# A graph network on one core: the turns of full chunks as transposing DMAs in place of TensorE's

## The reference

```python
h = jnp.maximum(_layernorm(x), 0.0)
x = x + _L0_gnn_ref(h, ...)     # 2 sage layers, then log_softmax
h = jnp.maximum(_layernorm(x), 0.0)
x = x + _L1_gnn_ref(h, ...)     # 2 sage layers, 2 linear layers

# layer of block 0:  agg = segment_sum(h[src], dst) / max(deg, 1)
#                    y = concatenate([h, agg]) @ W + b      128 -> 256 -> 128
# layer of block 1:  relu(mean @ W_l.T + b_l + x @ W_r.T)   128 -> 256 -> 256 -> 256 -> 128
```

## Time and profile before

| | |
|---|---|
| median of 3 runs | 588.14 us (587.84 to 588.85) |
| profiled execution | 587.56 us, span 585.7 us |
| PE | 544.2 us busy, 93% |
| DVE | 225.0 us, 38% |
| ACT | 202.9 us, 35% |
| SP's DMA queue | 27.91 MB, 17.6% of 16 DMA engines |

### The profile page before, as it was taken

One profiled execution on the slowest core, in us unless ns is written; L12 is line 12 of the kernel. 1 busy time (PEld: TensorE's weight loads), 2 busy tenths in 40 slices (PEclk: granted clock), 3 DMA queues, 4 the chain that ended last, 5 costly groups with the idle time before them and its releaser, 6 DMA issues.

```text
span 585.7 us, 9420 instructions
## 1 busy us (share of the span) xinstructions
PE 544.2 (93%) x3078; PEld 291.5 (50%) x3078; DVE 225.0 (38%) x500; ACT 202.9 (35%) x368; POOL 24.7 (4%) x36
## 2 busy tenths in 40 slices
PE   1367999999999999999999999999999999999996
PEld 0244655555554654445455555644545445454555
DVE  6899959577775217667411111110000001010001
ACT  1688858567664304455422222200000010100011
POOL 4410000000000000110100000000000000000000
PEclk9997999999999999999999999999999999999999
DMA  3800103010010124333121111232011212111011
GB/s 94 196 1 1 38 1 117 2 36 17 17 35 17 24 70 112 90 90 77 39 76 53 52 52 39 67 117 52 19 35 39 49 35 52 35 35 52 17 32 30
DMA packets 31372, 29.47 MB, mean 50 GB/s; under 512 B 4894, under 2 KB 30879, under 8 KB 31215
## 3 DMA queue, kind: packets, MB, share of 16 engines
q1 hardware_dynamic: 29622, 27.91, 17.6%
q10 hardware_dynamic: 1561, 0.84, 0.6%
q0 software_dynamic: 160, 0.33, 0.2%
HBM read 19.68 MB, written 9.39 MB: 50 GB/s over the span
## 4 chain that ended last, share of the span: by engine, by line
PE 87%; DVE 5%; ACT 3%; DMA 2%; issue 2%; POOL 1%; ACTq 0%; SPq 0%; DVEq 0%; POOLq 0%
PE ps L1036 54%; PE ps L1053 22%; PE ps L990 6%; PE ps L1308 2%; DVE hs_b L493 2%; PE ps L1046 1%; PE ps L1270 1%; DMA hs_b<-self_d 1%; DMA adj<-key_d,adj 1%; ACT adj L1490 1%; POOL adj L1375 1%; PE ps L1242 1%; DVE adj L1426 1%; DMA adj<-in_dst_dram 0%; ACT adj L844 0%
## 5 line engine op out<-in xcount | busy, mean ns | idle before, releaser
L1036 PE MATMUL ps<-adj,hs_b 125*128 (+2 forms) x1050 | 203.6, 351 | 0.0
L1036 PE MATMUL ps<-adj,hs_a 125*128 (+2 forms) x700 | 158.5, 353 | 0.0
L1036 PEld LDWEIGHTS ps<-adj,hs_b 125*128 125x128 f16 x1050 | 96.3, 97 | 103.9 <-issue 6.6
L493 DVE TENSOR_TENSOR hs_b<-iota,hs_b 128x1024 f16<-128x1024 f16 x150 | 95.4, 685 | 27.9 <-PE ps L990 26.9
L844 ACT ACTIVATE adj<-ps 125x500 f32 (+2 forms) x150 | 80.0, 544 | 22.8 <-PE ps L990 16.6
L990 PE MATMUL ps<-hs_b 128*128 128x125 f16 x625 | 68.5, 233 | 20.7 <-DVE hs_b L493 13.1
L990 PEld LDWEIGHTS ps<-hs_b 128*128 128x128 f16 x625 | 46.5, 103 | 65.7 <-DVE hs_b L493 34.4
L1036 PEld LDWEIGHTS ps<-adj,hs_a 125*128 125x128 f16 x700 | 58.5, 98 | 38.8 <-issue 5.4
L975 ACT ACTIVATE actT<-ps,col 128x500 f32<-128x500 f32 (+1 forms) x14 | 8.9, 633 | 148.0 <-PE ps L1053 148.0
L791 DVE TENSOR_TENSOR hs_a<-ps,hs_a 125x512 f32<-125x512 f32 (+1 forms) x7 | 4.4, 634 | 128.9 <-PE ps L1308 128.9
L1053 PE MATMUL ps<-aggT,wts 128*128 128x500 f32 (+1 forms) x112 | 44.6, 540 | 0.4 <-ACT aggT L957 0.4
(11 more groups left out here) (150 smaller groups left out, 356.4 us busy)
## 6 DMA issues: line engine op xcount, KB each, us to landing
invc<-inv_d SPq DMA_DIRECT2D x24, 250.0 KB, 3.3
h_d<-actT SPq DMA_DIRECT2D x6, 500.0 KB, 3.1
wts<-h_d SPq DMA_DIRECT2D x6, 500.0 KB, 4.0
self_d<-hs_b SPq DMA_DIRECT2D x6, 250.0 KB, 2.1
hs_b<-self_d SPq DMA_DIRECT2D x6, 250.0 KB, 3.5
hs_b<-in_x_dram SPq DMA_DIRECT2D x6, 250.0 KB
x_d<-hs_b SPq DMA_DIRECT2D x6, 250.0 KB
hs_a<-x_d SPq DMA_DIRECT2D x6, 250.0 KB
```

Source lines behind the costliest of these rows:

```text
L493: last = nc.vector.tensor_tensor(onehots[slot], iota2.unsqueeze(1).to_broadcast(shape), keys[:, ds(g * 4, 4), :].unsqueeze(2).to_broadcast ...
L1036: last = nc.tensor.matmul(acc[:, 0:n], hs[:, ds(s * (2 * w) + part * w + h * 128, 128)], adj[0:P, ds(c * (S * C) + s * n, n)], start=(isin ...
```

## The change

For the six full chunks of phases 1 and 3, PE, ACT and DVE lose the turns, and SP gets transposing DMAs (`dma_start_transpose`, 2-byte elements):

- Own rows: the rows are first stored to DRAM (`spread`: `hs_d1` in one piece at the start of phase 1; `hs_d3` chunk by chunk along phase 2). `turn_own` reads 512 rows of 128 high values, and 512 of 128 low values, and lands them turned in SBUF; DVE's `own_sum` adds the two into `aggT`. That of chunk c+1 is issued while chunk c is worked on, after `own_sum` of chunk c (one buffer).
- Projected rows of phase 1: ACT writes the high half as f16 into `z16[0]`, DVE the low half into `z16[1]` (`z_low`), and SP turns 4 tiles of 128x128 of each into `hs_b`: 8 DMAs per chunk.
- Activations of phase 3: ACT copies `actT` into a f16 buffer `h16` (2 instructions), SP turns it in 8 DMAs of 128x128; when these have landed DVE writes `actT - h16` into the same buffer, and SP turns that in 8 more. When those have landed, ACT may write the next chunk.

The small chunk 6 stays on PE. The waits for the rows in `source` become waits for the landings (`p1_zin`, `p3_in`).

```diff
+            def turn_own(ph, c, hd, into):
+                for k in range(2):
+                    sp.dma_start_transpose(into[k], hd[ds(c * C, 512), k * D:(k + 1) * D]).then_inc(sem(f"p{ph}_hT"), 16)
...
@@ SP, before the chunks of phase 1 @@
+            if not slow:
+                sp.wait_ge(sem("n_low"), S // PIECE)
             spread(1, ha, D, hs_d1)
             load_inv("p1_", 0, True)
+            if not slow:
+                sp.wait_ge(sem("rows"), 16)
+                turn_own(1, 0, hs_d1, turned1)
@@ SP, step1 @@
+                if not slow and nxt:
+                    sp.wait_ge(sem("p1_h0T"), c + 1)
+                    turn_own(1, c + 1, hs_d1, turned1)
                 sp.wait_ge(sem("p1_self"), c + 1)
                 sp.dma_start(self_d[:, ds(c * C, width(full))], selfT[:, 0:width(full)]).then_inc(sem("p1_self_out"), 16)
+                if not slow and full:
+                    sp.wait_ge(sem("p1_zlo"), c + 1)
+                    for t in range(4):
+                        for k in range(2):
+                            sp.dma_start_transpose(hs_b[:, ds(c * (4 * 2 * D) + (2 * t + k) * D, D)],
+                                                   z16[k][:, t * PT:(t + 1) * PT]).then_inc(sem("p1_zin"), 16)
...
@@ SP, phase 2, step2 and behind it @@
+                    sp.wait_ge(sem("p2_low"), c)
+                    sp.dma_start(hs_d3[ds((c - 1) * C, C), :].rearrange("(t p) f -> p t f", p=P),
+                                 ha[:, ds((c - 1) * (4 * 2 * D), 4 * 2 * D)].rearrange("p (t f) -> p t f", f=2 * D)).then_inc(
+                        sem("p2_rows"), 16)
...
+                sp.wait_ge(sem("p2_rows"), 16 * NFULL)
+                turn_own(3, 0, hs_d3, turned3)
...
@@ SP, step3 @@
+                if not slow and nxt:
+                    sp.wait_ge(sem("p3_ownT"), c + 1)
+                    turn_own(3, c + 1, hs_d3, turned3)
                 n = width(full)
                 sp.wait_ge(sem("p3_relu"), 2 * c + 2)
                 sp.dma_start(h3_d[:, :, ds(c * C, n)],
                              actT.rearrange("p (m n) -> p m n", m=2)[:, :, 0:n]).then_inc(sem("p3_h3_out"), 16)
+                if not slow and full:
+                    for k, half in enumerate(("p3_hi", "p3_lo")):
+                        sp.wait_ge(sem(half), c + 1)
+                        for t in range(4):
+                            for m in range(2):
+                                sp.dma_start_transpose(hs_b[:, ds(c * (4 * 2 * H) + (2 * t + k) * H + m * 128, 128)],
+                                                       h16[:, m, t, :]).then_inc(sem("p3_in"), 16)
...
@@ DVE @@
+            def own_sum(ph, c, parts):
+                dve.wait_ge(sem(f"p{ph}_hT"), 32 * c + 32)
+                wait_past(dve, "p1_h1" if ph == 1 else "p3_h3", 2 * c)
+                nc.vector.tensor_tensor(aggT[:, C:2 * C], parts[0][:, 0:C], parts[1][:, 0:C], ALU.add).then_inc(
+                    sem("p1_h0T" if ph == 1 else "p3_ownT"), 1)
...
                 agg_out(c - 1, True)
+                own_sum(1, c - 1, turned1)
...
                 self_out(c - 1, True)
+                z_low(c - 1)
...
             def low3(c, full):
+                if full and not slow:
+                    dve.wait_ge(sem("p3_in"), 256 * c + 128)
+                    for m in range(2):
+                        by_tile = h16[:, m, :, 0:P]
+                        last = nc.vector.tensor_tensor(by_tile, actT[:, m * C:(m + 1) * C].rearrange("p (t n) -> p t n", n=P),
+                                                       by_tile, ALU.subtract)
+                    last.then_inc(sem("p3_lo"), 1)
+                    return
@@ ACT, z_out and step3 @@
+                if full and not slow:
+                    wait_past(act, "p1_zin", 128 * c)
+                    nc.scalar.activation(z16[0].rearrange("p (t n) -> p t n", n=PT)[:, :, 0:P],
+                                         bank(6, n).rearrange("p (t n) -> p t n", n=P), ACT.Identity, scale=zs).then_inc(
+                        sem("p1_zT"), 1)
+                    return
...
+                if by_dma:
+                    act.wait_ge(sem("p3_relu"), 2 * c + 2)
+                    wait_past(act, "p3_in", 256 * c)
+                    for m in range(2):
+                        last = nc.scalar.activation(h16[:, m, :, 0:P], actT[:, m * C:(m + 1) * C].rearrange("p (t n) -> p t n", n=P),
+                                                    ACT.Copy)
+                    last.then_inc(sem("p3_hi"), 1)
+                    return
@@ PE @@
-                own1(c - 1, True)
...
-                turn1(c - 1, True)
...
-            staged(3, [(lambda c: bank(acc3(c, slow)), ha, D, 0)], [(0, own3, 1), (8, hidden3, 1), (0, turn3, 2)],
--                   [(14, turn2, NFULL)], (NFULL - 1, NFULL, NCH), fill=(5, 8))
+            staged(3, [(lambda c: bank(acc3(c, slow)), ha, D, 0)], ([(0, own3, 1)] if slow else []) + [(8, hidden3, 1)] + ([(0, turn3, 2)] if slow else []),
+                   [(14, turn2, NFULL)], (("p2_low", NFULL - 1), ("p2_low", NFULL), ("p2_low", NCH)), fill=(5, 8))
...
-                   [(0, own3, NFULL), (0, turn3, NFULL - 1), (8, hidden3, NFULL), (16, turn3, NFULL)],
-                   (2 * NFULL - 2, 2 * NFULL, 2 * NCH - 1))
+                   [(0, own3, NFULL), (8, hidden3, NFULL), (16, turn3, NFULL)],
+                   (("p3_in", 256 * (NFULL - 1)), ("p3_in", 256 * NFULL), ("p3_low", 1)))
```

More of the change, by code:

```diff
@@ L204, in sage_program @@
         outb = over(hs_a, 9216, 4 * D, F32)[0:P]
+        PT = 128
+        z16 = [zT[:, :].bitcast(F16)[:, k * 4 * PT:(k + 1) * 4 * PT] for k in range(2)]
+        turned1 = [hs_b[:, (20 + 2 * k) * 2 * D:(22 + 2 * k) * 2 * D] for k in range(2)]
+        turned3 = z16
+        h16 = wts[:, 512:1024].bitcast(F16).rearrange("p (m t n) -> p m t n", m=2, n=PT)
         w1v = wts[:, 0:512].rearrange("p (k o) -> p k o", k=2)
@@ L434, in phase @@
                 if slow:
-                    pool.wait_ge(sem(f"p{ph}_rows"), 16)
+                    pool.wait_ge(sem("rows"), 16 * ph)
                 def step(c, full):
@@ L646, in step1 @@
                     build_c(c + 1, nxt, 1, 5)
[L647 to L650 removed]
+                elif nxt is not None:
+                    build_c(c + 1, nxt, 0, 5)
                 self_out(c - 1, True)
+                z_low(c - 1)
                 if nxt is not None:
@@ L681, in dve_layers @@
                 agg_out(NFULL, False)
-                low(NFULL - 1, True)
                 self_out(NFULL, False)
@@ L760, in step3 @@
                     sem("p3_agg_out"), 1)
+                if full and not slow:
+                    own_sum(3, c, turned3)
                 if not first:
@@ L869, in z_out @@
                 act.wait_ge(sem("scale3"), 2)
-                wait_past(act, "p1_turned", c)
+                if full and not slow:
+                    wait_past(act, "p1_zin", 128 * c)
[3 more added lines that the diff above has]
+                    return
+                if slow:
+                    wait_past(act, "p1_turned", c)
+                else:
+                    act.wait_ge(sem("p1_zin"), 128 * NFULL)
                 nc.scalar.activation(zT[:, 0:n], bank(6, n), ACT.Identity, scale=zs).then_inc(sem("p1_zT"), 1)
@@ L883, in step1 @@
             def step1(c, full, nxt, second=False):
-                h0_turned(c - 1, True)
-                if not second:
-                    high(c - 2, True)
                 if nxt is not None:
@@ L927, in act_layers @@
                 step1(NFULL, False, None)
-                high(NFULL - 1, True)
                 whole(NFULL, False)
@@ L954, in step3 @@
                 nt = n // P
-                act.wait_ge(sem("p3_own"), c + 1)
-                wait_past(act, "p3_h3", 2 * c)
-                nc.scalar.activation(aggT[:, C:C + n], bank(3, n), ACT.Copy).then_inc(sem("p3_ownT"), 1)
-                wait_past(act, "p3_turned", 2 * c)
+                by_dma = full and not slow
+                if not by_dma:
+                    act.wait_ge(sem("p3_own"), c + 1 if slow else 1)
+                    wait_past(act, "p3_h3", 2 * c)
+                    nc.scalar.activation(aggT[:, C:C + n], bank(3, n), ACT.Copy).then_inc(sem("p3_ownT"), 1)
+                if slow:
+                    wait_past(act, "p3_turned", 2 * c)
+                else:
+                    wait_past(act, "p3_lo", c)
                 wait_past(act, "p3_h3_out", 16 * c)
@@ L1151, in step1 @@
                 pieces(S - 6, S).then_inc(sem("p1_agg"), 1)
-                if second:
-                    pe.wait_ge(sem("wt"), 5)
-                turn1(c - 1, True)
             if slow:
@@ L1165, in pe_layers @@
                 pe.wait_ge(sem("absw"), 2)
-                pe.wait_ge(sem("p1_rows"), 16)
+                pe.wait_ge(sem("rows"), 16)
                 chunks(pe, slow1)
@@ L1189, in slow_step, with ready @@
                         p(c, full)
+                def ready(k):
+                    name, value = source[k]
```

(9 more changed lines are left out.)

66 lines of the change are left out of this document (41 added, 25 removed).

## The result

The changed kernel takes 694.17 us (median of 4 runs, 692.62 to 697.55), the kernel before 588.50 in the same comparison (4 runs, 587.84 to 589.78): a ratio of 1.180, 95% interval 1.175 to 1.185. The forecast was 645 us and slower; the direction was right, most of the loss stands where it was put (phase 3), and the size was 49 us short.

The account below looks back on a forecast made before the run. PE, 93% busy, was taken to bound the kernel; six phase 3 laps of 22.7 us from 302.0 end at 438.2 against 381.5, so 587.6 + 56.7 = 644.3, given as 645 us; range 598 to 700.

Parts of the forecast that it names:

- PE's 13.9 us: Phase 3: PE's step once the turns are gone, 50 matmuls of 0.211 us plus 3.35 us of dense ones.
- The three rivals: Phase 3's turns: X 0.5 to 0.7 (chance 0.20); X below 0.48, faster (0.08); turns not overlapping, X = L (0.15).
- X: SP's queue: time from one transposing DMA's issue to the next, taken as 1.0 us, ends 0.51 and 1.25.
- The sign against the forecast: The forecast is wrong if PE stays above 90% busy in phase 3, or if the waits stand in phase 1.
- rival 3: Turns don't overlap, each waits for the one before to land: 726 us, 690 and up; chance 0.15.
- L: SP's queue: time from the last transposing issue to its landing, taken as 3.0 us, ends 2.1 and 4.5.
- SP's other work between laps lies beside L and the high copies: Phase 3: inverse, two row turns and the store of actT, about 3 us, were to add nothing to a lap.
- the start of the first lap: Phase 3: first lap starts at 302.0, moved from 300.7 by -6.3 + 5.8 + 1.8 = +1.3 us.
- The 6.3 us off PE in phase 1: Phase 1: own-row and projected-row turns leaving PE save 6.3 us, bounds 5.3 and 8.
- phase 2 to 3: 0: Between phases 2 and 3: chunk 5's row store, two turns and own_sum eat the 0.44 us gained, no more.
- The +1.8 at phase 1's end: End of phase 1: PE's turn of chunk 6 waits for zT behind chunk 5's turns, 213.9 against 212.1.
- some us: Phase 3: a waiting PE can drop to half clock, its 13.9 us becoming 27.8; some us on the upper side.

Follow-up runs that it names:

- e1: The changed kernel with phase 1's turns done by PE as in the kernel before; 673.26 us.
- e2: The changed kernel with phase 3's turns back on PE and no row store in phase 2; 610.30 us.
- e4: The changed kernel with each half of phase 3's activations stored to DRAM, then turned by four 512 x 128 DMAs in place of sixteen per chunk; 617.97 us.
- e7: The changed kernel with phase 3's own rows turned by PE as before and no row store in phase 2; 680.86 us.
- e3: The changed kernel with each row store of full chunks issued as two DMAs, 112 and 13 partitions, in place of one of 125; 683.59 us.
- b8: b6 plus phase 1's turns by DMA, chunk 0's own rows left on PE, row store split and issued behind the inverse loads; 599.46 us.
- b6: The kernel before with 512 x 128 DMA turns of activations for chunks 0 to 4, two accumulator banks, low halves ahead of the aggregate's eviction; 590.17 us.

## Why the prediction was right and wrong

**Right: the mechanism.** The one buffer h16 makes laps of copy, 8 issues, landing, subtraction, 8 issues, landing; the laps outlast PE's 13.9 us and set the end. e1 and e2 put 85 of 107 us on phase 3, e4 gives 76 back by cutting the number of issues. PE waits for the DMA out of wts between phases 3 and 4 (16.6 us) and at tile 20 (6.2), as named. The three rivals' mechanisms are out: X is neither 0.5 to 0.7 nor below 0.48, and turns do overlap (X 1.28 against a landing of 2.3). The sign against the forecast, waits in phase 1, came true in part: 21.1 of the 104.9 us were there at phase 1's last dense layer (230.74 against 209.63).

**Luck: the range.** The forecast proper was X 0.7 to 1.25 and 616 to 689 us, with a chance of 0.54. Neither X = 1.28 nor 694 us lies in it; 694 lies in the band given to rival 3 (690 us and up). The range to 700 held it because some room had been added for that rival. With X and L as measured the forecast's own sum gives about 660 us; the other 34 are the two failed terms below and the clock.

**Mis-sized: X and L.** I took X = 1.0, from the 0.99 of ACT's finely cut load, and L = 3.0. The turns start 1.28 us apart, just over my upper end of 1.25, and land 2.3 us after the issue. 14 x 0.28 - 2 x 0.7 = +2.5 on the lap: 25.2. Nearest was not that row but the other end, POOL's indirect DMAs at 1.25. The Trainium skill (VectorE: DVE Perf Modes, "The three transpose paths") gives 1309 ns for a 128x128 turn by DMA; the trace has 1.28 us, 2% off. The Trainium skill's rule that transposing DMAs are as fast as regular ones (Advanced Engine Details and Errata, "X-Bar Transpose (TRN2)") does not hold for issue here: SP's plain issues in the lap above last 0.35 and 0.59 us, a turn 1.14. It holds for latency, 2.3 us against a median of 2.1 for a plain store.

**Failed: "SP's other work between laps lies beside L and the high copies".** It doesn't. From the start of the last issue, landing and high copies take 3.4 us, so the next lap could have begun at 406.7 (high copies from 405.60, 1.13 us). SP was at its inverse load, two own-row turns and store from 405.01 to 408.81, and the next lap's first turn left at 408.95, 2.2 us late. e7 shows it, 25.05 against 27.3. What stood in SP's program between two laps counted as soon as it outlasted landing and copies. Over six laps, the sizes of X and L (15.1) and this term (8.7) are (160.0 - 136.2) = 23.8 of the 48 us by which the last landing was misplaced (160.0: high copies of chunk 0 at 326.4 to the last landing at 486.4).

**Failed: the start of the first lap, +25.7 in place of +1.3.** The other 24.4 us are the largest miss, in four parts.
The row store was priced at the 279 GB/s that small packets had reached, 7.7 us with latency; it took 16.9. That figure was a rate of many DMAs at once; this was one DMA of 125 partitions. e3 gives 10.6 us back. The store was also issued 2.3 us later than said (64.29).
DVE resumed its groups at 85.71 in place of 68.89, and waited not only at own_sum, as said, but longer at the eviction ahead of it, whose inverse landed behind the row store:

```profile
81.80 0.68 DVE L660 TENSOR_TENSOR aggT<-ps,invc 128x500 f32<-128x500 f32 x1 [12.17 <-DMA invc<-inv_d]
85.12 0.68 DVE L671 TENSOR_TENSOR aggT<-hs_b 128x500 f32<-128x500 f16 x1 [2.64 <-DMA hs_b<-hs_d]
85.71 1.89 DVE L538 TENSOR_TENSOR hs_b<-iota,hs_b 128x1024 f16<-128x1024 f16 x3
```

I had named what waits behind own_sum, but not what stands behind the store in SP's queue and shares its DMA engines.
The 6.3 us off PE in phase 1 never became time: from the first hidden layer to the last dense one the lateness even grew, from 17.6 to 21.1 us. A step of 25.7 us has 24.1 us of PE in it, where it was 24.9 of 25.3: PE's turns went, the step did not get shorter. DVE is 70% busy there and I called own_sum hidden by that share; but it stands between an eviction and the one-hots that PE needs next, and b8 shows the same waits without the store.
Last, "phase 2 to 3: 0" was some +2.5, with PE waiting 2.70 us at the first third hidden layer: the row store of chunk 5 took 5.9 us in place of 3.1, then turn, landing and own_sum. The +1.8 at phase 1's end held: PE waited 2.35 us for zT at the turn of chunk 6.

**The clock.** The forecast put "some us" on a PE that waits. Phase 3 ran at 0.78 of full speed, a mixture of its two levels, 1.2 and 2.4 GHz: the 16 matmuls after a wait of 11.44 us took 5.44 us in place of 3.54:

```profile
382.04 5.44 PE L1122 MATMUL ps<-adj,hs_a 125*128 x16 [11.44 <-DVE aggT L825]
```

Within phase 3 this cost nothing more, since PE was not the bound. Behind tile 20 it was, and there the lower clock cost 2.8 us; b6 shows the same on a smaller scale, 5.28 us in place of 3.52 behind a 2.44 us wait.

## What to carry to other kernels

A transposing DMA was paid per instruction here, not per byte (128x128 out of SBUF against 512 x 128 out of DRAM): count the issues on the queue that carries them, add all else that this queue carries, and turn 512 rows at a time, if need be by way of DRAM. Before taking work off a busy engine, look at what it covers: PE's turns stood where PE would have waited for an eviction, and only with a second accumulator bank did the freed time come back. When a DMA that something waits for is put in front of others, price it by its own shape and name who waits for those behind it.
